# A cross-attention kernel on one core: new orders in the queues of SyncE, GpSimd, ScalarE, VectorE and TensorE, and the low parts of y's tiles 1 to 3 made last

## What is computed

```python
x_q = jnp.einsum('oc,bcn->bno', w_qk, y)
x_k = jnp.einsum('oc,bcn->bon', w_qk, x)
x_v = jnp.einsum('oc,bcn->bon', w_v, x) + b_v[None, :, None]
energy = jnp.einsum('bnc,bcm->bnm', x_q, x_k)
attention = jax.nn.softmax(energy, axis=-1)
attention = attention / (1e-07 + attention.sum(axis=1, keepdims=True))
x_r = jnp.einsum('bcn,bnm->bcm', x_v, attention)
x_r = jax.nn.relu(jnp.einsum('oc,bcn->bon', w_t, x - x_r) + b_t[None, :, None])
return x + x_r
```

## Time and profile before

| | us |
|---|---|
| median of 3 runs | 2077.18 (2074.06 to 2080.71) |
| profiled execution | 2079.49 |
| its span, first to last instruction | 2077.7 |
| TensorE busy (matmuls) | 1912.0 (92%) |
| VectorE busy | 1682.2 (81%) |
| ScalarE busy | 1409.7 (68%) |
| GpSimd busy | 1074.4 (52%) |
| mean granted clock of TensorE | 0.961 |

### The profile page before, as it was taken

The page is one execution under the profiler, slowest core; times in us unless marked ns, Lnnn a source line. Parts: engine busy times, 40 slices in busy tenths (PEclk is TensorE's granted clock), DMA queues, the critical chain, the costliest instruction groups (busy, mean ns, idle before and its releaser), DMA issues.

```text
span 2077.7 us, 27090 instructions
## 1 busy us (share of the span) xinstructions
PE 1912.0 (92%) x8808; PEld 1574.1 (76%) x8808; DVE 1682.2 (81%) x2096; ACT 1409.7 (68%) x1990; POOL 1074.4 (52%) x583
## 2 busy tenths in 40 slices
PE   5999999999999998999999999999999999999999
PEld 4778777787777787777877778777778777777777
DVE  3878878788878888888788878888887888888877
ACT  3777666776667776676766777666777667776665
POOL 5445555455544545554555545564454554455541
PEclk7999999999999999999999999999999999999999
DMA  4034422344222443223442234432244413344211
GB/s 132 26 102 122 122 61 85 97 121 121 75 87 81 121 121 109 62 81 111 121 121 62 93 88 121 121 95 70 78 121 121 120 52 104 88 121 121 82 40 61
DMA packets 78240, 199.50 MB, mean 96 GB/s; under 512 B 8688, under 2 KB 9712, under 8 KB 78192
## 3 DMA queue, kind: packets, MB, share of 16 engines
q1 hardware_dynamic: 60544, 166.10, 22.6%
q0 software_dynamic: 17360, 32.51, 9.7%
q10 hardware_dynamic: 288, 0.39, 0.1%
HBM read 149.16 MB, written 33.55 MB: 88 GB/s over the span
## 4 chain that ended last, share of the span: by engine, by line
PE 45%; issue 19%; ACT 19%; POOL 11%; DVE 3%; DMA 2%; ACTq 0%; SPq 0%; DVEq 0%; POOLq 0%
PE pv L974 16%; POOL xt_lo L256 8%; PE row_b L836 6%; PE row_a L836 4%; PE row_b L932 4%; PE row_a L932 4%; ACT p_sb L445 4%; PE row_b L888 4%; ACT p_hi L453 4%; PE row_a L888 3%; ACT x_hi L357 3%; PE pv L946 3%; ACT ev L436 2%; DVE res L729 2%; ACT x_sb L371 2%
## 5 line engine op out<-in xcount | busy, mean ns | idle before, releaser
L288 POOL TENSOR_TENSOR y_lo<-y_raw,y_hi 128x896 fp32r<-128x896 f32 (+1 forms) x128 | 283.0, 2233 | 394.9 <-DVE p_lo L678 270.9
L671 DVE SCALAR_TENSOR_TENSOR colsum<-p_sb,row_inv,colsum 128x1024 f32<-128x1024 f32 x224 | 402.4, 1797 | 8.3 <-DVE row_inv L659 0.4
L678 DVE SCALAR_TENSOR_TENSOR p_lo<-p_sb,row_inv,p_hi 128x1024 fp32r<-128x1024 f32 x254 | 326.8, 1302 | 78.3 <-ACT p_hi L453 77.7
L234 POOL TENSOR_TENSOR x_lo<-x_raw,x_hi 128x1024 fp32r<-128x1024 f32 x62 | 151.4, 2441 | 435.7 <-ACT x_hi L357 435.7
L445 ACT ACTIVATE p_sb<-p_sb,neg_max 128x1024 f32<-128x1024 f32 x256 | 293.3, 1149 | 55.0 <-DVE neg_max L651 55.0
L436 ACT ACTIVATE ev<-row_b 128x512 f32<-128x512 f32 x384 | 228.4, 595 | 139.6 <-PE row_b L836 139.0
L453 ACT ACTIVATE p_hi<-p_sb,row_inv 128x1024 fp32r<-128x1024 f32 x256 | 293.0, 1145 | 43.8 <-PE pv L974 43.8
L974 PE MATMUL pv<-p_hi,z_lo 128*128 128x512 f32 x1024 | 295.5, 413 | 0.0
L974 PE MATMUL pv<-p_hi,z_hi 128*128 128x512 f32 x1024 | 281.7, 392 | 14.6 <-DVE res L729 14.4
L974 PE MATMUL pv<-p_lo,z_hi 128*128 128x512 f32 (+1 forms) x1047 | 273.4, 384 | 0.0
L651 DVE CUSTOM_DVE_ANT_0 p_sb<-row_a,ev 128x1024 f32<-128x1024 f32 x128 | 156.5, 1223 | 135.5 <-PE row_a L836 135.1
(11 more groups left out here) (192 smaller groups left out, 4126.4 us busy)
## 6 DMA issues: line engine op xcount, KB each, us to landing
x_sb<-x SPq DMA_DIRECT2D x64, 512.0 KB, 5.9
xt_raw<-x SPq DMA_DIRECT2D x124, 256.0 KB, 5.2
x_raw<-x SPq DMA_DIRECT2D x62, 512.0 KB, 7.1
out<-res SPq DMA_DIRECT2D x62, 512.0 KB, 3.4
y_raw<-y SPq DMA_DIRECT2D x64, 256.0 KB, 4.0
y_raw<-y SPq DMA_DIRECT2D x32, 512.0 KB, 3.8
xt_raw<-x POOLq DMA_DIRECT2D x31, 512.0 KB, 5.4
xt_raw<-xt_raw POOLq DMA_DIRECT2D x62, 256.0 KB, 6.2
```

The source lines that it names most:

```text
L234: nc.gpsimd.tensor_tensor(x_lo[par][:, kt, :], raw, x_hi[par][:, kt, :].bitcast(FP32), ALU.subtract).then_inc(x_lo_done, 1)
L288: nc.gpsimd.tensor_tensor(y_lo[:, of:, cols], y_raw[:, 1 + of:8, cols], y_hi[:, of:, cols].bitcast(FP32), ALU.subtract).then_inc(y_lo_done, 1)
L671: nc.vector.scalar_tensor_tensor(out=colsum[:, :], in0=p_sb[r][:, :], scalar=inv, in1=colsum[:, :], op0=ALU.mult, op1=ALU.add).then_inc(ac ...
L678: nc.vector.scalar_tensor_tensor(out=p_lo[r][:, :], in0=p_sb[r][:, :], scalar=row_inv[:, j:j + 1], in1=p_hi[r][:, :].bitcast(FP32), op0=AL ...
```

## The change

SyncE loads xt first and y behind it. On GpSimd, y_sums goes ahead of xt_one (but in batch 0), y_low(b + 1, 0) and xt_four follow xt_two, the low parts of xt and x alternate by halves, the wait for p_lo_done is gone, and y_low(b + 1, 1 to 3) come last, behind t_low, where batch b + 1's first slot begins. g_operands is cut in two. On ScalarE, xt_high(0) goes ahead of x_high in slot 2, xt_high(1) to the end of slot 2, the second x_bias to slot 3, y_high(b + 1, 2) and gx_high_one between the gx passes. On VectorE, gx_add (cut in two) and gx_parts go ahead of the last p_low, which is called inside gx_parts behind T_2N; col_inverse is cut in two with no change of order. On TensorE, gx_p1 waits only for the first half of x_lo, gx_p2 for the second, and the first z_half no longer waits for all of gx_lo.

```diff
             def batch(b, par, first=False, last=False):
                 if not last:
+                    if not first:
+                        sp.wait_ge(gx21_full, b)
+                    load_xt(b + 1)
                     sp.wait_ge(y_hi_done, NP * (b + 1))
                     sp.wait_ge(y_lo_done, NP * (b + 1))
                     load_y(b + 1)
-                    if not first:
-                        sp.wait_ge(gx21_full, b)
-                    load_xt(b + 1)
...
             def batch(b, par, last=False):
                 if not last:
-                    xt_one(b + 1)
+                    if b == 0:
+                        xt_one(b + 1)
+                        g_operands()
                     y_sums(b + 1)
+                    if b > 0:
+                        xt_one(b + 1)
                     xt_two(b + 1)
+                    if b > 0:
+                        y_low(b + 1, 0)
+                    xt_four(b + 1)
                     if b == 0:
-                        g_operands()
-                    y_low(b + 1, 0)
-                    xt_four(b + 1)
-                    for kt in range(KT):
-                        x_low(b + 1, 1 - par, kt)
+                        g_operands_low()
+                        y_low(b + 1, 0)
                     for h in range(2):
                         xt_low(b + 1, h)
-                    pool.wait_ge(p_lo_done, NT * (b + 1))
-                    for t in range(1, NP):
-                        y_low(b + 1, t)
+                        x_low(b + 1, 1 - par, h)
                     t_three(b + 1)
                     t_low(b + 1, 0)
                     t_low(b + 1, 1)
+                    for t in range(1, NP):
+                        y_low(b + 1, t)
...
                 if t >= 2 and not last:
+                    if t == 2:
+                        xt_high(b + 1, 0)
                     x_high(b + 1, 1 - par, t - 2, early=first)
-                    xt_high(b + 1, t - 2)
                 copy_b(b, t, 2, EV_U3, 1.0)
...
-                if 0 < t < 3 and not first and (t == 2 or not last):
-                    x_bias(b, t - 1)
+                if t == 1 and not first and not last:
+                    x_bias(b, 0)
+                if t == (2 if last else 3) and not first:
+                    x_bias(b, 1)
...
                 if t == 2 and not last and not first:
                     y_high(b + 1, 1)
+                if t == 2 and not last:
+                    xt_high(b + 1, 1)
...
                 if t == NP - 1 and not last:
                     gx_pass(b + 1, gx11, gx22, gx22_part, 3 * b + 1, -1.0)
+                    y_high(b + 1, 2)
                     gx_pass(b + 1, ev[:, 3, :], gx12, gx12_part, b + 1, 1.0)
                     gx_pass(b + 1, ev[:, 2, :], gx22, gx22_part, 3 * b + 2, 1.0)
+                    gx_high_one(b + 1)
...
-                    gx_high_one(b + 1)
                     gx_pass(b + 1, gx21, gx22, gx22_part, 3 * b + 3, -1.0)
-                    y_high(b + 1, 2)
                     y_high(b + 1, 3)
...
                 if b < B - 1 and t == NP - 1:
                     turn(b)
-                if b < B - 1 or t < NP - 1:
+                    gx_add_one(b + 1)
+                    gx_add_two(b + 1)
+                    gx_parts(b + 1, before_low=lambda: p_low(b, t, 1))
+                elif b < B - 1 or t < NP - 1:
                     p_low(b, t, 1)
...
             def gx_p1(b, par):
-                pe.wait_ge(x_lo_done, KT * (b + 1))
+                pe.wait_ge(x_lo_done, KT * b + 1)
...
-            def gx_p2(par):
+            def gx_p2(b, par):
+                pe.wait_ge(x_lo_done, KT * (b + 1))
...
-                    pe.wait_ge(gx_lo_done, 3 * (b + 2))
+                    pe.wait_ge(gx_lo_done, 3 * (b + 1) + 1)
+                    pe.wait_ge(t_made, 3 * (b + 1) + 1)
                     z_half(1 - par, 0)
+                    pe.wait_ge(gx_lo_done, 3 * (b + 2))
                     z_half(1 - par, 1)
```

More of the change, by code:

```diff
@@ L271, in g_operands, with g_operands_low @@
                 nc.gpsimd.tensor_tensor(ns4, g12, ns2, ALU.subtract).then_inc(g_summed, 1)
+            def g_operands_low():
+                sums = g_sums
                 pool.wait_ge(gs_hi_done, 1)
@@ L496, in pair @@
                     y_high(0, 3, first=True)
-                if t == 0 and first:
+                if t == 1 and first:
                     g_operands_high()
@@ L597, in gx_add, with gx_add_two, gx_parts @@
                 nc.vector.tensor_tensor(gx12, gx12, ev[:, 2, :], ALU.add).then_inc(gx_added, 1)
+            def gx_add_two(b):
                 dve.wait_ge(gx_passed, 4 * b)
                 nc.vector.tensor_tensor(gx22, gx22, ev[:, 3, :], ALU.add).then_inc(gx_added, 1)
-            def gx_parts(b, first=False):
+            def gx_parts(b, first=False, before_low=None):
                 b_low(b, 0, B_11, row_b[:, left], 1)
@@ L780, in batch @@
                     col_inverse(b)
+                    spread(b)
                     return
-                gx_add(b + 1)
-                gx_parts(b + 1)
                 col_inverse(b)
+                spread(b)
                 scale(b, 0)
```

8 lines of the change are left out of this document (5 added, 3 removed).

## The result

The changed kernel takes 2092.11 us (2085.18 to 2096.95), 1.0049 times the kernel before, with an interval of 1.0025 to 1.0073: slower by half a per cent, where 2175 was forecast. The sign was right, the size was not. The profiled execution took 2092.8, 13.3 more than that of before. The first product of batch 1 now starts at 85.58 instead of 103.95, 18.4 earlier; that of batch 31 at 2035.15, 13.3 later. So two things were added up: batch 0 is 18.4 shorter, and the 30 batches from 1 to 30 are (2035.15 - 85.58) / 30 = 64.99 long each, 1.06 more than 63.93, 31.7 together.

A forecast was written before the change was run, and what follows sets the result against it. TensorE's 3.5 us wait for xt_lo and 2.5 of half rate a batch were taken as the prize. Period 47.0 + 18.7 + 1.5 = 67.2 against 63.93, times 30, is +98: 2177 profiled, 2175 median; range 2010 to 2229.

The forecast's parts named there:

- The term for batch 0: Batch 0 has no y chain of this kind, so its time was to change by 0, within 3 us.
- the parts (a): ScalarE's slots 2 and 3, GpSimd's alternating low parts: remove TensorE's wait before gx_p5, about 3.5 us a batch.
- The third rival: New order works throughout, no wait replaces the one before gx_p5: period 58.3 us, time 1908; chance 0.08.
- The moved y_low up to y_sums: Late y_low delay SyncE's load_y to 5.3 us behind the batch's first product; the third load lands at 10.5.
- Three turns ... T+19.1: GpSimd's y_sums lose three port turns to VectorE, last 8.6 us, end 19.1 us behind the batch's first product.
- y_high at 19.2, then the exponent at 21.6, then TensorE's stalls: ScalarE's y_high waits for y_sums; exponent starts at 21.6 instead of 19.4; TensorE stalls 0.3 and 1.6 us.
- y_low(b + 1, 0) at 25.6 takes the port ahead of both p_low, 30.2: GpSimd's y_low takes the port for 2.1 us at 25.6; VectorE's two p_low follow, reaching 30.2.
- The cluster, last energy_out of tile 3 at 47.0: Four low parts, two column sums, two p_low share the port by turns, 14.4 us; tile 3's energy_out end at 47.0.
- A new stall of about 3.5 in place of the one removed: TensorE's gx_p1 waits about 3.5 us for tile 3's energy_out, replacing the removed wait.
- 18.7 behind it, and 1.5 for the clock: VectorE's chain after tile 3's energy_out takes 18.7 us to the batch's end; half-rate clock adds 1.5 a batch.
- the first (VectorE keeps the port): Rival: VectorE holds the port through back-to-back instructions, gx_p1 doesn't wait; period about 62.0, time 2019 us; chance 0.22.
- The second (turns half and half, 63.4 to 64.9): Rival: x_low(1) comes just behind the last p_low, energy_out ends at 44.7; 2061 to 2106 us; chance 0.15.

The follow-up runs named there:

- experiment 1: Kernel before, only the order in batch 0 changed: g_operands first on GpSimd, g_operands_high in slot 1: 2061.01 us, 0.9904 of before.
- experiment 5: Changed kernel with ScalarE's y_high(b + 1, 0) moved behind the first p_high of slot 1: 2092.99 us, 1.0057 of the kernel before.
- experiment 4: Changed kernel with each x_low and xt_low (but batch 0's first) replaced by two plain writes of zeros: 1942.87 us, 0.9346 of the kernel before.
- experiment 7: Changed kernel with xt_one ahead of y_sums and y_high(b + 1, 0) behind slot 1's first p_high: 1987.08 us, 0.9542 of the kernel before.
- experiment 2: Changed kernel with y_low of tiles 1 to 3 put back ahead of t_three: 1962.2 us, 0.9442 of the kernel before.
- experiment 6: Changed kernel with xt_one ahead of y_sums on GpSimd: 2092.67 us, 1.005 of the kernel before.
- experiment 3: Changed kernel, xt_four's DMA replaced by a short write: 2075.8 us; kernel before, small GpSimd DMA added ahead of xt_low: 2079.46; one place earlier: 2067.6.
- experiment 9: Changed kernel with y_low of tiles 1 to 3 ahead of t_three, plus xt_high(b + 1, 0) at the end of slot 1: 2000.49 us, 0.9589 of before.
- experiment 8: Kernel before with y_low of tiles 1 to 3 behind t_low: 2256.97 us, 1.0815; second run also loads xt ahead of y: 2203.11, 1.0582.

## Why the forecast had the sign and not the size

In short: three steps failed. The term for batch 0, put at nothing, was -18.4 (experiment 1). The first energy_out of tile 2 was put at 30.2, behind ScalarE's late y_high and behind a y_low that goes ahead of both p_low; it came at 28.0 in the mean, since y_sums were 1.2 quicker, the chain through y_high carried no time (experiment 5), and y_low went ahead of one p_low only, in 13 of 30 batches. And the stretch behind tile 3, the clock included, was put 0.8 too long. What did carry the time is the port, as forecast: VectorE's contending instructions, 205 us longer in all (experiments 4 and 7). That the sign came out right rests on 31.7 us in 30 batches against the 18.4 that nobody had counted, so there is some luck in it.

- **What bounds the kernel before, and what the parts (a) gain:** right in kind. The wait for xt_lo is gone in every version with the new orders; they bring the period from 63.93 to 60.70 (experiment 2). The third rival's 58.3 was not reached even so: a wait of gx_p1 (2.1 a batch) and some half rate (1.0) are left there.
- **"Batch 0 ... 0, within 3": wrong, -18.4.** The step said that batch 0 has no y chain of this kind; true, but the change moved g_operands and ScalarE's g_operands_high there (the latter stands in the edit of experiment 1 and not in the diff printed ahead), and the sum did not price them. The wait of 21.1 was in the trace.
- **The moved y_low up to y_sums:** right. Load issued at T+5.3 (5.5 forecast), y_sums start at 10.6 (10.5).
- **"Three turns ... T+19.1":** 17.9. y_sums lasted 7.4 and not 8.6: the turns added 1.4 to the 6.0 of before, not 2.6. I take it that one of them fell into the pause ahead of the last sum; no run separates it.
- **y_high at 19.2, then the exponent at 21.6, then TensorE's stalls:** y_high came at 17.9, and ScalarE's wait was 3.1 a batch, as forecast. But the batch is no shorter without it (experiment 5). This link of the chain was wrong in the changed kernel: VectorE itself was as late. It holds where the wait is 5.5 (experiments 6 and 7).
- **y_low(b + 1, 0) at 25.6 takes the port ahead of both p_low, 30.2:** 28.0 in the mean. xt_one landed after 7.4, not 5.4, so GpSimd came at 27.2 in the batch shown (1084.19), when the pair at 1082.10 was almost through. In 13 of the 30 batches y_low did get the port ahead of the second p_low, as forecast, and tile 2 started at 28.5 to 30.4; in the other 17 it came too late and tile 2 started at 26.1 to 27.7. These 17 are the ones in which a column sum then takes over 8 us, and in both kinds the last energy_out of tile 3 ends near 45.6 (45.9 and 45.4 in the mean).
- **The cluster, last energy_out of tile 3 at 47.0:** 45.6. The mechanism is shown by experiment 4: without these turns it is 40.6 and the period 60.20. From the first energy_out of tile 2 to here I took 16.8, and it is 17.6; with the 2.2 by which tile 2 starts earlier that makes the -1.4.
- **"A new stall of about 3.5 in place of the one removed":** half right. It stands as drawn (3.0 a time, 30 times) in experiment 3. In the changed kernel 19 column sums of tile 2 take over 7 us, p_high of the tile waits for row_inv (ACT p_hi <- DVE row_inv, 78.4 us in 19), and TensorE's wait moves ahead to copy_e, 73.5 us in 19.
- **18.7 behind it, and 1.5 for the clock:** 64.99 - 45.6 = 19.4 against 20.2: -0.8. Half rate costs 1.8 a batch (109 us of it, half of that lost, in 30 batches); how much of that lies in this stretch I did not separate.
- **The sum:** -1.4 and -0.8 are the 2.2 between 67.2 and 65.0, 66 us over 30 batches; with the 18.4 of batch 0 this is the 85 between 2177.6 and the profiled 2092.8, or in medians the 83 between 2175 and 2092. Small terms each; but what is left of a gain of 3.2 and a loss of 4.3 a batch is 1.1, and beside that they decide the size.
- **The rivals:** the first (VectorE keeps the port) falls by the 13 pairs of p_lo that gave way between the two, and by the 8.51. The second (turns half and half, 63.4 to 64.9) is nearer in time, with energy_out at 44.7 where 45.6 was measured; its reason, x_low(1) coming behind the last p_low, is seen in the batch shown (1099.54), but there it is a column sum that waited through three low parts.

The rule of the Trainium skill, "SBUF — State Buffer", section "Who interferes with whom", that the one that issues first holds the lock for its whole instruction, agrees with what one instruction does here (3.03). Who is next was read from the rows, and the forecast's "one that waits gets the port ahead of the holder's next" has an exception, below.

Open: why 1987 is still 25 us above 1962 (0.83 a batch); how the 149 us of experiment 4 divide between the port and GpSimd's shorter work; what decides, beside a GpSimd DMA under way, whether VectorE is passed over; and whether a transfer that SyncE issues does the same. No run was made for any of these.

## What to carry to other kernels

Price every call that a diff moves in the first iteration as well: one wait of 21 us there gave back 18.4 of the 31.7 us that 30 batches lost. Where a late load holds up two engines at once, taking one engine's wait away may show nothing: follow the busy and idle time of the engine that both paths end on (VectorE here) and undo the causes together. And before a stall is removed, look at which engine it had held back: in experiment 9 TensorE ran into another, and the kernel became slower.

## What the runs showed of the hardware

- A VectorE instruction with two inputs in SBUF that finds GpSimd at work gets its turn between two of GpSimd's instructions (62 of 62 in the kernel before, 3.03 and 3.17 for 1.28 of work). If it arrives while a DMA that GpSimd has issued is under way, it can be passed over until GpSimd has nothing at hand: 6.26 to 6.30 in 31 of 31 in experiment 3, 8.1 to 9.0 in 17 batches of the changed kernel, though that DMA lands after 3.3 us, ahead of the last of these changes of instruction. When the small DMA of experiment 3 had landed before the arrival, the turns were back (3.04 and 3.17). At low parts this never came without such a DMA (0 of 265) and not always with one (73 of 99, experiment 3); what decides is open. The kernel before with y_low last (experiment 8, first run) has it with other instructions: in 29 of 30 batches a p_lo takes 4.6 to 6.0, passed over by y_sums while xt_one's DMA is under way.
- The issue alone does not hold the port: in the kernel before, column sums that start during a DMA issue with no low part behind it take 1.28.
- GpSimd's plain writes hold up neither a column sum nor a p_lo: the 123 that lie beside nothing else of GpSimd's in experiment 4 take 1.27 to 1.29, and with writes in place of the four low parts the port time fell from 934.4 to 726.5.
- xt_one's transfer of 512 KB, which adds in place, landed after 5.4 us in the kernel before, 7.4 in the changed one and 8.9 beside y's loads (experiment 6), whose parts of 256 KB then took 5.6 instead of 3.8.
